# Unread products on constants in two waits of TensorE in the cross-attention stage of a decoder layer

## The reference

```python
x = x + self_attention(layernorm(x))     # mask: blocks of 64 tokens + 8 global tokens
x = x + cross_attention(layernorm(x), ctx)   # 64 context tokens, then relu(out @ W1 + b1) @ W2 + b2
x = x + experts(layernorm(x))            # top 2 of 16 experts with sigmoid gates, plus a shared expert
```

```python
q = (x @ Wq + bq); k = (y @ Wk + bk); v = (y @ Wv + bv)      # per head
attn = softmax(q k^T / sqrt(8))
h = relu((attn v) @ W1 + b1);  return h @ W2 + b2
```

## Time and profile before

| | us |
|---|---|
| median of 3 runs | 781.0 (776.43 to 783.17) |
| the profiled execution, device time | 782.83 |
| its span, first to last instruction | 780.8 |
| mean granted TensorE clock | 0.889 |
| PE busy, DVE busy | 591.2, 495.7 |
| ACT busy, POOL busy | 288.7, 330.2 |

### The profile page before, as it was taken

How to read it: one execution, slowest core, us unless ns; L and a number is a source line. 1 busy time by engine, 2 the same in 40 slices (tenths; PEclk the granted TensorE clock), 3 DMA queues, 4 the chain that set the end, 5 groups by cost and what they waited for, 6 DMA issues and landing times. The chain is left out here.

```text
span 780.8 us, 17864 instructions
## 1 busy us (share of the span) xinstructions
PE 591.2 (76%) x5275; PEld 392.6 (50%) x5276; DVE 495.7 (63%) x1390; ACT 288.7 (37%) x812; POOL 330.2 (42%) x628
## 2 busy tenths in 40 slices
PE   4775888888888888778778887875667876777772
PEld 3554666566665665344434444453335654655441
DVE  8564677886778766689798888874422332232367
ACT  2523444454444542144333434432223433343110
POOL 7531333323233231116565766765424544454100
PEclk9976999999999998699889889987877897797997
DMA  5785344335433533513231322320222222222343
GB/s 156 119 286 77 77 78 60 73 78 83 68 60 72 79 75 73 135 47 81 62 95 52 96 61 74 82 68 17 91 56 69 75 72 76 67 82 64 122 121 94
DMA packets 95331, 65.85 MB, mean 84 GB/s; under 512 B 24752, under 2 KB 90624, under 8 KB 95296
## 3 DMA queue, kind: packets, MB, share of 16 engines
q1 hardware_dynamic: 90688, 55.44, 31.7%
q0 software_dynamic: 4608, 9.97, 4.0%
HBM read 20.54 MB, written 17.56 MB: 49 GB/s over the span
## 5 line engine op out<-in xcount | busy, mean ns | idle before, releaser
L573 POOL DMA_INDIRECT expert_out<-ey,xt x80 | 77.5, 969 | 91.7 <-DVE ey L878 74.8
L968 ACT ACTIVATE probs<-ps 128x512 f32<-128x512 f32 x128 | 73.1, 596 | 64.0 <-PE ps L1364 31.9
L630 DVE TENSOR_REDUCE nmax<-ps 128x8 f32<-128x512 f32 x128 | 81.2, 683 | 19.4 <-PE ps L1226 11.8
L873 DVE TENSOR_TENSOR eh<-ps,sg 128x128 f32<-128x128 f32 x80 | 23.3, 291 | 105.2 <-ACT sg L1090 81.8
L549 POOL DMA_INDIRECT expert_in<-xn,sloti x64 | 64.5, 1008 | 27.4 <-issue 14.6
L1195 PE MATMUL ps<-probs,constants 128*32 128x256 f32 x512 | 72.5, 429 | 0.0
L649 DVE RECIPROCAL rden<-ps 128x256 f32<-128x256 f32 x32 | 56.2, 1756 | 21.4 <-PE ps L1195 16.1
L1457 PE MATMUL ps<-wgu,xtT 128*128 x160 | 66.6, 506 | 2.0 <-ACT xtT L1084 1.5
L442 POOL TENSOR_SCALAR veps<-mv 128x2 f32<-128x2 f32 x48 | 10.7, 224 | 119.5 <-issue 84.2
L1450 PE MATMUL ps<-constants,xt 128*128 128x128 f32 x80 | 27.9, 349 | 38.1 <-issue 22.0
L1364 PE MATMUL ps<-qs,ckbd 128*128 128x256 bf16 x128 | 25.9, 311 | 23.3 <-DVE qs L645 10.7
(11 more groups left out here) (207 smaller groups left out, 1442.8 us busy)
## 6 DMA issues: line engine op xcount, KB each, us to landing
qs<-part SPq DMA_DIRECT2D x192, 64.0 KB, 3.4
kbd<-part SPq DMA_DIRECT2D x96, 128.0 KB, 3.9
xt<-expert_in SPq DMA_DIRECT2D x80, 72.0 KB
ck_scr<-wgu SPq DMA_DIRECT2D x6, 512.0 KB, 4.5
ckbd<-ck_scr SPq DMA_DIRECT2D x16, 192.0 KB
expert_in<-zero_rows SPq DMA_DIRECT2D x32, 72.0 KB
wgu<-in_L_ffn_gate_up_w SPq DMA_DIRECT2D x1, 2048.0 KB, 9.6
cvbd<-cvbd_all SPq DMA_DIRECT2D x16, 128.0 KB
```

Of the source, the lines that this page charges most:

```text
L573: pool.indirect_dma_start(ys, bass.IndirectOffsetOnAxis(xt[p][:, E:E + 1].bitcast(I32), 0), ey[p % 4][:, :], None).then_inc(e_(f"out{p % 4 ...
L630: v.tensor_reduce(nmax[:, u, 8 * half:8 * half + 8], bank[:, :].rearrange("p (h k) -> p h k", k=64), AX.X, ALU.max, negate=True).then_inc( ...
L968: a_.activation(probs[:, 2 * i:2 * i + 2, :], P2[i % 2][:, :].rearrange("p (j q) -> p j q", j=2), ACT.Exp, scale=SCALE).then_inc(s("probs" ...
```

## The change

A helper `keep_busy(bank, n)` issues n products of 128 x 128 weights and 256 columns, both bf16 and both from the constant tile `aheadb`, into the first 256 columns of a bank. Nothing reads what they write, and the products behind them overwrite it. Five stand at the head of `cross_hidden`, before its wait for attT, in MISC; seven stand before pair(0), behind a wait for exponentials of the sequence before, in P2[0]. No wait, no DMA and no other instruction changes.

```diff
             if "B" in phases:
+                def keep_busy(bank, n):
+
+                    for _ in range(n):
+                        mm(bank[:, 0:256], aheadb[:, 0:128], aheadb[:, :], start=True, stop=True)
+
                 def cross_hidden(b):
+                    keep_busy(MISC, 5)
                     pe.wait_ge(c_("attT"), b + 1)
@@
                     values = lambda n, j: cvbd[p][:, j, :]
                     at_least(pe, c_("probs"), 4 * b)
+                    keep_busy(P2[0], 7)
                     pair(0)
                     pair(1)
                     pe.wait_ge(c_("probs"), 4 * b + 1)
```

## The result

| | before | after |
|---|---|---|
| median of 4 runs, us | 781.4 (776.4 to 783.2) | 806.1 (805.7 to 808.2) |
| ratio, 95% interval | | 1.033 (1.028 to 1.038) |
| span of the profiled execution, us | 780.8 | 803.8 |

The changed kernel is 3.3% slower; 770 us (765 to 782) had been forecast. In the changed kernel the products added stand at L1303, the hidden products at L1309, the pairs at L1370, the counts' first product at L1335. L649, L968, L1191 and L1195 have kept their numbers.

A forecast was written before the change was run, and what follows sets the result against it. It took cross-stage bodies as bound by VectorE at 12.75 us, or by TensorE when half speed covers the weigh products. Gains 4.35 + 6.1 + 1.0 + 0.7 less 0.9 gave 11.25 us: 770 us, range 765 to 782.

The forecast's parts named there:

- Three more cold bodies: Cross stage: VectorE's waits for weigh products in three slow bodies, 6.3 us, of which 6.1 us would be returned.
- a chance of other lateness: Unpriced remainder, counted with the slower rival in the 0.11 chance of a slower kernel.
- the clock holds at 1.00: Sign in the trace after: granted clock in the cross stage 0.97 or more, against 0.87.
- rival 1: Cross stage: filled waits still don't hold the clock; 782 us, or 776 if half of it held; chance 0.17.
- The products' own length: Added products on TensorE: five before the attT wait 0.55 us, seven before pair(0) 0.77 us, 0.16 more with the tail.
- the six bodies from 411.38 to 492.69: Cross stage: VectorE's waits for weigh products before its reciprocals in six bodies, 4.35 us to be gained.
- a floor of 12.75: Cross-stage body: bound by VectorE at 12.75 us when the clock holds.
- The 1.0 us of the first body: First cross-stage body: seven products raise the clock for its second half only, 1.0 us net gain, between -0.4 and 2.
- "same": Whole kernel: measured time within 1% of the kernel before, chance 0.34.
- Rival 2: Cross stage: waits for scatters to land eat the gain, 9 us come back, 779 us; chance 0.13.
- Rival 3: Cross stage: clock falls over hidden products and scores instead, about 1.8 us a body against 0.75, 791 us; chance 0.10.
- Rival 4: Added products: weight loads and products run in series, seven last 1.5 us, five 1.05; 774 us; chance 0.03.

The follow-up runs named there:

- r_after: The changed kernel run again unaltered, against the kernel before on the same chip: 765.8 us, ratio 0.997.
- each repeat: Any of four later runs of the unaltered changed kernel, on three chips, against the kernel before: ratios 0.994 to 0.997.
- r_before: The kernel before run again unaltered, against itself on the same chip: 769.5 us, ratio 1.003.
- e2_sevens: The changed kernel with only the seven products before pair(0), the five left out, against the kernel before: 768.1 us, ratio 1.003.
- r_after_third: The changed kernel run unaltered once more, against the kernel before on the same chip: 767.2 us, ratio 0.996.
- e4_written_out: The changed kernel with all 16 cross-stage bodies written out, no loop, against the kernel before: 763.6 us, ratio 0.991.
- e7_late_exp_after: The changed kernel with one more exponential ahead of the first in the ten looped bodies, against the kernel before: 782.1 us, ratio 1.014.
- e9_later_exp_after: The changed kernel with two more exponentials ahead of the first in the ten looped bodies, against the kernel before: 802.5 us, ratio 1.045.
- e8: The kernel before with one more exponential ahead of the first in the ten looped bodies, against it without: 799.5 us, ratio 1.038.

## Why the prediction was wrong

**Step that failed for the first measurement.** "Three more cold bodies end at 342.66, 383.12 and 411.38 with waits of 1.62, 2.79 and 1.90: 6.3 us, of which PE can return nearly all (I take 6.1)". Two of the three waits (at 383.12 and 411.38) were not a clock that fell in short gaps but exponentials that came 1.8 us after their pairs; the third, 1.62 us at 342.66, was of the kind I took it for, and the body gained 1.7 us. I took all three for the same kind and did not follow the waits back to ScalarE. The same holds for the slow body in the earlier trace rows: its second exponential was 1.8 us late (434.75). Lateness of this kind was in the profile in five of ten looped bodies, had no place among the rivals beyond "a chance of other lateness" without a price, and in the changed kernel it struck ten of ten. What the runs showed in its place: a pause of 2.9 us behind the first pairs, then 6.8 us at half speed, so that the body takes 17.03 us, up to 3.9 over r_after's 13.17, and the loop 162.6 us against r_after's 132.2. Why the completions came late stays open.

**What held.** With no exponential late the clock holds at 1.00 with both groups of products in eight or nine of the ten looped bodies of each repeat, against two of ten in r_before (rival 1 falls), and in five of the six written-out bodies even in the first measurement (-5.7 us over six bodies). The products' own length came out as worked (0.71 and 0.92 us), in the first after trace the hidden ones still waited for VectorE's attT (0.19 us), pair(0) for the shift copies. The Trainium skill, "TensorE: Matmul & The Clock Gate", section "HAM oscillation — how this bites in real kernels", has the clock fall in long waits for DMA between bursts of products. The bodies of r_before at 0.87, whose waits at these two places are 0.54 and 0.76 us, and those of r_after at 1.00 show that short waits lower it as well, and that filling them keeps it up in most bodies.

**The term that was too large without lateness.** "... the six bodies from 411.38 to 492.69 have 0.68, 0.83, 0.69, 0.75, 0.68 and 0.72 (first, second and last in the rows): 4.35 us", down to a floor of 12.75. On the other chips the looped bodies went from 13.5 to 13.17, so six of them gave 2.0 us. VectorE waited for 0.7 us in two bodies, and its busy time rose from 11.89 to 12.13 us a body; three of its instructions that the last section tells of took 1.77 and 1.98 us instead of 1.58 to 1.62. The floor was read from one body, and it holds for written-out bodies (12.73) and not in the loop. With VectorE busy 12.10 us in the one and 12.13 in the other, the 0.4 us between them lie between its instructions. Of the 6.1 us, 1.6 came (the body at 342.66; in the repeats it went from 13.6 to 11.6 or 11.9 us). The rest had nothing to come from: r_before has one body of such a wait in the loop (14.65 us), and the repeats have their own of 14.5 us and more. The 1.0 us of the first body can't be told: it took 15.4 to 16.6 us in five traces of the changed kernel and 15.2 to 17.9 in five without products. So the change is worth 0.3 to 0.6% there (the intervals go from -0.1 to 0.9), not 1.4%, within what had been called "same".

**Rival 2** (the scatters eat the gain) did not come: in the looped bodies of the repeats VectorE waited for no scatter, and for 0.5 to 0.8 us in the fourth written-out body. **Rival 3** is what the 14.5 us bodies are: it struck one or two of ten, at 1.3 us a body over 13.17, and four or five of ten without the five (e2_sevens). A body of 17.4 us in r_after_third has both falls, over the hidden products and over the weigh products. **Rival 4** fell with the seven's 0.92 us, within which their loads (0.75 us in the first after trace) ran too. The rule of the Trainium skill that it goes by stands in the section "The mechanism" of "TensorE: Matmul & The Clock Gate", not in the one that the prediction names.

**Behind the cross stage** 5.1 us were lost in the first measurement; in the repeats that part took 242.3 us before and 241.4 to 244.3 after. So there the kernel before, too, was 6.5 us slower in the first measurement (248.8), in a part that the change doesn't touch. This was not isolated.

## What to carry to other kernels

Where a profile has the same instruction come late in some bodies and not in others, follow that wait back before costing anything by those bodies; if its releaser is not known, it belongs among the rivals, with the price of all bodies being struck. Filling two short waits of TensorE held its clock in eight or nine of ten bodies, where filling one only moved the fall to the next stretch in four or five. And a gain that depends on the clock is capped by the next engine's body as it is in the loop, which is to be read from looped bodies, several of them.

## What the runs showed of the hardware

- The pairs' completions reached ScalarE 1.1 to 2.4 us late in some bodies of both kernels in one measurement, in none of 18 runs after it, with records of increments missing around them; the kernel before took 781 us there and 769 to 770 on the four chips of the experiments.
- A pause of 2.49 us of TensorE between the pairs was followed by 3.4 us at half speed in nine of ten bodies, one of 2.93 us, once it had recurred, by 6.8 us (e7_late_exp_after, e9_later_exp_after): 0.44 us more pause made the looped body 1.5 to 1.9 us longer and the kernel 20 us.
- With a pause of 2.49 us in ten bodies the kernel with the products took 782 us, the one without 799.5 (e7, e8); in the traces half of the difference in the cross stage lies in the ten bodies, whose clock fell for 3.4 us with the products and mostly for 6.8 without.
- In most looped bodies one of three VectorE instructions on 128 x 256 elements lasts two to four times as long as it does elsewhere: L623 in seven bodies of r_before (0.87 to 0.92 us against 0.42), L619 (1.05 against 0.42) or L621 (1.14 against 0.29) by turns in r_after. The three together take 1.58 to 1.62 us there, 1.77 or 1.98 here, and 1.97 to 1.99 in most bodies of e4_written_out. What holds them up was not tried.
